# Experts' output bias moved from seventeen small products into the open block sums, as one 24-row product per block

## The chip, the cores and the metric

The kernel runs on one core of one Trainium2 chip. The metric is the device time of one execution in microseconds; the median of three runs of the kernel before is 252.2 us. The core has five engines that run their own instruction queues and wait for each other by semaphores: TensorE (PE, matrix products into the eight banks of PSUM), VectorE (DVE), ScalarE (ACT), GpSimd (POOL) and SyncE (SP), which here only issues transfers. ScalarE and GpSimd issue transfers as well, each on a queue of its own.

## What is computed

A vision transformer block over 32 images: a patch embedding with perturbed weights, a class token, attention with relative positions, and a mixture of eight experts of which each token uses the two with the highest probability. This part matters here (`comb` has one weight for each token and expert, zero for all but two):

```
logits = xf @ Wr.T + br
probs = jax.nn.softmax(logits, axis=-1)
top2_prob, top2_idx = jax.lax.top_k(probs, 2)
comb = jnp.zeros((n, e), x.dtype).at[jnp.arange(n)[:, None], top2_idx].add(top2_prob)
h = jax.nn.gelu(jnp.einsum('nd,edh->enh', xf, W1) + b1[:, None, :], approximate=False)
o = jnp.einsum('enh,ehd->end', h, W2) + b2[:, None, :]
y = jnp.einsum('ne,end->nd', comb, o)
```

The experts' output bias therefore adds `comb @ b2` to each token, a product of (tokens x 8) by (8 x 128). There are 2080 tokens: 2048 patches and 32 class tokens.

## The kernel before

Every engine's program is written out by hand, in the order in which it runs; the order around the change is the order of the calls in the source.

The experts run in two ways. Experts 0 and 1 are "direct". `up(e, blk)` makes the hidden units of one block of 416 tokens (five blocks, `FB` = 416, six products: each operand is split into a rounded high part and a low rest, and three of the four products are taken, for two halves of the hidden units). ScalarE applies the gelu. `down(e, g)` multiplies back for a group of four tiles of 128 tokens (five groups, the last one the class tokens), and DVE adds the result, weighted with the token's weight, to the accumulator `acc` in SBUF (L1286). Each such accumulation counts up `acc_ok`.

Experts 2 to 7 are summed in PSUM. For each of 30 steps (a block and an expert, `STEPS`), PE runs `up`, ScalarE the gelu (`lift`, L760), DVE multiplies the hidden units with the token weights (`weigh`, L1260), ScalarE rounds them to the high part (`rounded`, L768), DVE takes the low rest (`rest`, L1269), and PE adds six products to the block's open sum (`down_sum`), two steps behind the `up`. A sum stays open in bank 4 or 5 over the six experts of a block. ScalarE then copies it out, PE turns it back (`turn_back`, L1836) and DVE adds it to `acc` (`joined`, L1307), after which SyncE and ScalarE write the output.

`weigh` needs each token's weight on all 128 partitions. For that DVE computes the weights `comb` (L1231), PE turns them (`L1789`, after `comb_ok` and the first two accumulations), ScalarE copies them to `combT` and signals `cT_ok`, SyncE and ScalarE write six rows of 2080 weights to a scratch area in the output tensor, and SyncE reads them back with each row repeated over the partitions: one transfer of 208 KB for each expert of block 0 (counted by `d_we2` to `d_we6`), and for each later block one of 832 KB (experts 2 to 5, into `region_c`) and two of 208 KB (expert 6 into `xnT`, expert 7 into `QT`). Block 1's three are counted by `d_wb1`; those of blocks 2, 3 and 4 are counted together, and `weigh` waits for all nine of them:

```
if blk:
    dve.wait_ge(S[f"d_wb{min(blk, 2)}"], 48 if blk == 1 else 3 * 48)
```

The output bias is handled apart. PE forms it from the turned weights with products of 8 rows (`base` in PE's program: sixteen of 128 x 128 between `up(2, 0)` and `up(3, 0)`, one for the class tokens after `up(3, 0)`), into banks that later groups need too, and DVE adds it to `acc` in five instructions (L1239, L1242), before expert 0's last group. In the profile each such product is recorded as two passes, and so is each product of `down`. PE's first open sum waits for all fifteen accumulations, since its banks are among those of the groups.

GpSimd has nothing to do after it has made the second layer norm's scales (L532).

Of the kernel before, what the change touches and what calls it, by code (L numbers as in the profile page):

```python
# [24 lines left out]
E = 8  # L25
# [16 lines left out]
G_RING, H_RING = 4, 6  # L42
BACK = [range(0, 3), range(3, 6), range(6, 9), range(9, 13), range(13, 16)]
# [4 lines left out]
K_ALL = 672  # L48
# [16 lines left out]
def constants():  # L65
# [17 lines left out]
    k[:, K_PRIO:K_PRIO + E] = E - np.arange(E)[None, :]  # L83
    return k


def vit_kernel(nc, consts, x, cls_tok, W1_w, W1_b, W1_sw, W1_sb, W2_w, W2_b, W2_sw, W2_sb, W3_w, W3_b,
               eps_in1, eps_out1, eps_in2, eps_out2, Wq, bq, Wk, bk, Wv, bv, Wo, bo, rel_k, rel_v,
               Wr, br, fW1, fb1, fW2, fb2, out):
    with ExitStack() as ctx:  # L90
# [61 lines left out]
        b2s = sb("b2s", C)  # L152
        clsr = sb("clsr", C)
# [66 lines left out]
        accT = region_d[:, 0:ALL]  # L220

# [15 lines left out]
        names = """d_we2 d_we3 d_we4 d_we6 w2hi_ok w2lo_ok d_cs d_wb1 d_wb2 hs_ok hi_ok lo_ok y3_ps at_ok tb_ps fin_ok nm1_ok nmr1_ok xnA_ok d_const d_const2 d_eo d_w1b d_rows d_bias d_w1 d_w2 d_x0 d_x1 d_x2 d_small d_rel d_rvd d_attn d_ffn d_fw1 d_out d_out2 w1hi_ok w1_split  # L237
# [6 lines left out]
        lg_ok lexp_ok comb_ok cT_ps cT_ok base_ps acc_ok h_ps gelu_ok y2_ps cz_ok lz_ok cb_ok xn2D_ok h0o_ok d_h0s d_h0q nm_ok nmr_ok relkb_ok dve_c dve_m act_c  # L244
# [26 lines left out]
        def out_expert(e, g):  # L271

            n = 5 * e + g
            return n if n < AHEAD else n + 7

        def out_base(c):
            return AHEAD + 2 + c
# [35 lines left out]
        def _(sp_):  # L313
# [66 lines left out]
            sp_.wait_ge(S["d_out"], 16 * 18)  # L380

        @block.gpsimd
        def _(pool):
# [18 lines left out]
            for c in range(4):  # L402
                g.dma_start(b2s[32 * c:32 * c + E, :], fb2).then_inc(S["d_small"], 16)
# [36 lines left out]
            pool.wait_ge(S["d_small"], 112)  # L440
# [85 lines left out]
            g.tensor_tensor(w1_lo[:, :], w1_sb[:, :], w1_hi[:, :].bitcast(F32), ALU.subtract).then_inc(S["w1_split"], 1)  # L526
# [15 lines left out]
            deviation2(4)  # L542

        @block.scalar
        def _(act):
# [244 lines left out]
            for f in range(2, 4):  # L790
                a.dma_start(oq[f][:, tt, :], acc[32 * f:32 * f + 32, tt, :]).then_inc(S["d_out2"], 16)
            act.wait_ge(S["fin_ok"], 6)
            a.dma_start(out[:, 0, :], acc[0:IMG, PAIRS, :]).then_inc(S["d_out2"], 16)
            act.wait_ge(S["d_out2"], 48)

        @block.vector
        def _(dve):
# [69 lines left out]
            dve.wait_ge(S["d_small"], 112)  # L867
# [364 lines left out]
            accv = KT[:, 0:TOK].rearrange("p (g c d) -> p g c d", g=4, c=4)  # L1232

            def base(u):

                dve.wait_ge(S["base_ps"], 1 + u // 4)
                dve.wait_ge(S["acc_ok"], AHEAD)
                if u < 4:
                    v.tensor_tensor(accv[:, :, u], bank[out_bank(out_base(u))].rearrange("p (g d) -> p g d", g=4),  # L1239
                                    accv[:, :, u], ALU.add).then_inc(S["acc_ok"], 1)  # L1240
                else:
                    v.tensor_tensor(acc[0:IMG, PAIRS, :], bank[out_bank(out_base(u))][0:IMG, 0:C], acc[0:IMG, PAIRS, :],  # L1242
                                    ALU.add).then_inc(S["acc_ok"], 1)
# [27 lines left out]
            for e in range(DIRECT):  # L1271
                for g, tiles in enumerate(GROUPS):
                    u = out_expert(e, g)
                    if (e, g) == (0, AHEAD):
                        for c in range(5):
                            base(c)
# [3 lines left out]
                    if e > 0:  # L1280
                        dve.wait_ge(S["acc_ok"], max(AHEAD + 5, out_done(out_expert(e - 1, tiles[0] // 4))))
                    elif g >= AHEAD:
                        dve.wait_ge(S["acc_ok"], AHEAD + 5)
# [6 lines left out]
                    if (e, g) == (1, 2):  # L1290
                        weigh(0)
                        weigh(1)
                    if (e, g) == (1, 3):
                        weigh(2)
                        rest(0)
# [576 lines left out]
```

## Time and profile before

| | |
|---|---|
| measured, three runs | 252.07, 252.2, 254.18 us |
| median | 252.2 us |
| span of the profiled execution, first to last instruction | 249.9 us |
| time around that span | not in the profile |
| PE busy | 230.9 us, 92% of the span |
| DVE busy | 191.3 us, 77% |
| ACT busy | 164.2 us, 66% |
| POOL busy | 62.8 us, 25% |
| granted clock of PE | 1.00 of full speed throughout |

An engine's share is a mean over stages that differ. The last 90 us, from the token weights on, are the stage of the change. PE's records overlap, since products are pipelined: what one costs PE is the step from one start to the next, not its own length.

### The profile page before, as it was taken

To read this page: it belongs to the slowest core of one execution; us is meant where nothing else is said; L and a number is where in the kernel's file an instruction comes from. 1 tells how busy PE (TensorE), PEld (TensorE's weight loads), DVE (VectorE), ACT (ScalarE), POOL (GpSimd) and SP (SyncE) were. 2 spreads that over 40 slices of the span, in tenths; PEclk is the share of its full clock that TensorE was granted. 3 is DMA by queue.
4 is the path that set the end of the run, shared out by engine and by line. 5 is a ranking of instruction groups with operands and counts; after the bars stand their busy time and mean duration, and the time that the engine had idled before them with its cause. 6 is when DMAs were issued, how large, how long until landed. Compare 5 with 4: busy or idle time off the path is not lost.

```text
span 249.9 us, 6298 instructions
## 1 busy us (share of the span) xinstructions
PE 230.9 (92%) x2316; PEld 194.7 (78%) x2316; DVE 191.3 (77%) x481; ACT 164.2 (66%) x509; POOL 62.8 (25%) x94
## 2 busy tenths in 40 slices
PE   1999999999998889989989999999899999999993
PEld 1945665899776766658778899889799999999972
DVE  1576789865668899998186738678999989989991
ACT  2461469752199899993026987422799888898870
POOL 8814132096005465469112400000000000000000
PEclk9999999999999999999999999999999999999999
DMA  6980000000003326064000000069888510001011
GB/s 147 335 217 3 1 0 1 3 3 0 3 0 81 91 65 108 4 212 129 3 7 3 0 3 0 8 103 131 151 211 260 173 37 10 22 4 32 0 42 34
DMA packets 15625, 16.46 MB, mean 66 GB/s; under 512 B 1747, under 2 KB 14367, under 8 KB 15468
## 3 DMA queue, kind: packets, MB, share of 16 engines
q1 hardware_dynamic: 14424, 15.59, 26.0%
q0 software_dynamic: 544, 0.35, 0.6%
q8 instruction: 18, 0.29, 0.5%
q10 hardware_dynamic: 628, 0.14, 0.3%
q14 instruction: 11, 0.09, 0.1%
HBM read 13.91 MB, written 2.16 MB: 64 GB/s over the span
## 4 chain that ended last, share of the span: by engine, by line
PE 54%; DVE 13%; issue 11%; POOL 11%; DMA 4%; ACT 3%; SPq 2%; DVEq 0%; POOLq 0%
PE banks L1328 49%; POOL region_e L471 5%; DMA region_d<-in_L_tok_W_sw 4%; DVE KT L1286 2%; POOL w_lo L526 2%; DVE top L1028 1%; DVE stb L992 1%; POOL region_d L478 1%; PE banks L1531 1%; POOL rstd L413 1%; PE banks L1672 1%; DVE stb L911 1%; ACT region_d L701 1%; DVE y_lo L1269 1%; DVE stats L890 1%
## 5 line engine op out<-in xcount | busy, mean ns | idle before, releaser
L760 ACT ACTIVATE w_sb<-banks,vecs 128x416 f32<-128x416 f32 x60 | 36.4, 608 | 11.2 <-PE banks L1328 8.9
L677 ACT ACTIVATE region_e<-banks,ntop 128x64 f32<-128x64 f32 x128 | 38.3, 346 | 5.0 <-DVE ntop L1035 4.8
L768 ACT ACTIVATE y_hi<-w_sb 128x416 fp32r<-128x416 f32 x60 | 32.7, 548 | 8.1 <-DVE w_sb L1260 8.1
L1269 DVE TENSOR_TENSOR y_lo<-w_sb,y_hi 128x416 fp32r<-128x416 f32 x60 | 34.9, 585 | 1.0 <-ACT y_hi L768 1.0
L677 ACT ACTIVATION_READ_ACCUMULATOR region_e<-banks,ntop 128x1 f32 x128 | 29.8, 238 | 0.0
L1328 PE MATMUL banks<-x_hi,w_hi 128*128 128x416 f32 x80 | 29.3, 366 | 0.0
L1328 PE MATMUL banks<-x_lo,w_hi 128*128 128x416 f32 x80 | 28.1, 352 | 0.0
L1328 PE MATMUL banks<-x_hi,w_lo 128*128 128x416 f32 x80 | 28.0, 350 | 0.0
L1260 DVE TENSOR_TENSOR w_sb<-w_sb,region_c 128x416 f32<-128x416 f32 x40 | 23.4, 586 | 2.5 <-ACT w_sb L760 1.0
L1328 PE MATMUL banks<-y_hi,w_hi 128*128 128x416 f32 x60 | 22.3, 371 | 1.5 <-DVE KT L1286 1.0
L1328 PE MATMUL banks<-y_hi,w_lo 128*128 128x416 f32 x60 | 21.1, 351 | 0.0
L1328 PE MATMUL banks<-y_lo,w_hi 128*128 128x416 f32 x60 | 21.0, 351 | 0.0
L1328 PE MATMUL banks<-kc 128*128 128x128 f32 x76 | 14.1, 316 | 5.6 <-DMA kc<-in_consts 5.6
L471 POOL TENSOR_TENSOR region_e<-region_e,rsum 128x512 f32<-128x512 f32 (+1 forms) x15 | 15.5, 1032 | 7.6 <-DVE ntop L1035 5.6
L1328 PEld LDWEIGHTS banks<-kc 128*128 128x128 f32 x76 | 11.1, 212 | 6.7 <-DMA kc<-in_consts 5.6
L1328 PE MATMUL banks<-w_all,region_d 128*128 128x128 f32 (+1 forms) x136 | 16.3, 277 | 0.0
L1328 PEld LDWEIGHTS banks<-x_hi,w_hi 128*128 128x128 f32 x80 | 15.0, 188 | 1.3 <-DVE x_lo L1168 0.6
L1328 PEld LDWEIGHTS banks<-w_all,region_d 128*128 128x128 f32 (+1 forms) x136 | 15.5, 187 | 0.6 <-ACT w_sb L760 0.2
L1328 PE MATMUL banks<-region_d,relk_bd 64*128 64x64 f32 x256 | 15.3, 288 | 0.0
L1328 PEld LDWEIGHTS banks<-x_lo,w_hi 128*128 128x128 f32 x80 | 15.0, 187 | 0.3
L1328 PEld LDWEIGHTS banks<-x_hi,w_lo 128*128 128x128 f32 x80 | 15.0, 188 | 0.1
L1328 PEld LDWEIGHTS banks<-region_d,relk_bd 64*128 64x128 f32 x256 | 14.6, 188 | 0.6 <-issue 0.5
(238 smaller groups left out, 502.1 us busy)
## 6 DMA issues: line engine op xcount, KB each, us to landing
region_c<-out SPq DMA_DIRECT2D x4, 832.0 KB, 14.3
xnT<-out SPq DMA_DIRECT2D x5, 208.0 KB, 13.7
QT<-out SPq DMA_DIRECT2D x5, 208.0 KB, 14.1
region_a<-in_x SPq DMA_DIRECT2D x2, 512.0 KB, 5.3
region_a<-in_x SPq DMA_DIRECT2D x1, 1024.0 KB, 9.5
out<-h SPq DMA_DIRECT2D x2, 512.0 KB, 5.8
h<-out SPq DMA_DIRECT2D x4, 256.0 KB, 5.0
w_sb<-in_L_ffn_W SPq DMA_DIRECT2D x1, 1024.0 KB, 5.6
```

The lines of the kernel that those rows point to most:

```text
L413: g.tensor_tensor(rstd[:, n * TPB:(n + 1) * TPB], ve[:, n * TPB:(n + 1) * TPB], mhalf[:, :], ALU.pow).then_inc(S["rstd_ok"], 1)
L471: g.tensor_tensor(ev, ev, rv, ALU.mult).then_inc(S["pn_ok"], 1)
L478: g.tensor_copy(pc_rep[:, 2 * (u % 2):2 * (u % 2) + 2, :, :].rearrange("p r h d -> p (r h) d"), PcA[:, 16 * u:16 * u + 16].unsqueeze(2).to ...
L526: g.tensor_tensor(w1_lo[:, :], w1_sb[:, :], w1_hi[:, :].bitcast(F32), ALU.subtract).then_inc(S["w1_split"], 1)
L677: last = a.activation(dst[:, h // 2, h % 2], src[:, h // 2, h % 2], ACT.Exp, scale=SCALE, bias=ntop[:, o + h:o + h + 1], accum_out=esum[:, ...
L701: a.activation(HB[:, e % 2, s, blk * FB:(blk + 1) * FB], bank[h_bank(i)][:, 0:FB], ACT.Gelu, bias=vecs[:, v:v + 1]).then_inc(S["gelu_ok"], 1)
L760: a.activation(lifted(u), bank[h_bank(i)][:, 0:FB], ACT.Gelu, bias=vecs[:, b:b + 1])\
L768: a.activation(h_hi(u), lifted(u), ACT.Copy).then_inc(S["hi_ok"], 1)
L1260: v.tensor_tensor(lifted(u), lifted(u), weights(e)[:, blk * FB:(blk + 1) * FB], ALU.mult)\
L1269: v.tensor_tensor(h_lo(u), lifted(u), h_hi(u).bitcast(F32), ALU.subtract).then_inc(S["lo_ok"], 1)
L1286: last = v.scalar_tensor_tensor(acc[0:m, t, :], bank[out_bank(u)][0:m, i * C:(i + 1) * C], comb[0:m, t, e:e + 1], acc[0:m, t, :], op0=ALU. ...
L1328: return t_.matmul(o, l, r, start=start, stop=stop)
```

## The change

The seventeen bias products, DVE's five additions and their counts go. In their place each block's open sum gets one more product at its end, with 24 rows and 416 columns: the turned weights of the block's tokens (24 rows) by the bias (24 rows by 128). The 24 rows are three times the eight experts, so that the product in the rounded format is as exact as the others: rounded weights by rounded bias, rounded weights by the bias's rest, the weights' rest by the (rounded) bias.

- GpSimd builds the 24 rows of the bias (`b2r`) after its last old work. One added column of the constant table holds the signs for that.
- GpSimd splits the token weights next to `comb`, in place: rounded weights twice, then the rest. PE's transposes now wait for that (`cs_ok`) instead of for `comb_ok`; they turn the 24 new columns along with the eight old ones, so their number stays.
- After `y2_ps` has reached 7 (group 1 of expert 1 is through PE), GpSimd writes the 24 turned rows to the scratch area in five transfers, waits, reads them back in one transfer as 24 rows of 2080 (`crow`), waits, and casts the rows of each block into one of three buffers (`share`).
- PE waits for the block's cast before the added product (`split_ok`).
- With the bias banks gone, the groups use their banks in a new order, expert 1 waits for fewer accumulations, the first open sum waits for the accumulation of expert 1's group 2 in place of the last one, and DVE's first weighings and rests move forward by one group.
- At the end SyncE waits for all 21 output transfers; ScalarE no longer waits for its own three.

The core of the diff:

```diff
-            for c in range(4):
-                g.dma_start(b2s[32 * c:32 * c + E, :], fb2).then_inc(S["d_small"], 16)
+            for c in range(3):
+                g.dma_start(b2s[E * c:E * c + E, :], fb2).then_inc(S["d_small"], 16)
...
+            link(g.tensor_copy(b2t, b2s[0:3 * E, :]))
+            link(g.tensor_scalar(b2n, b2t.bitcast(F32), kc[0:3 * E, K_NM:K_NM + 1], None, ALU.mult))
+            g.tensor_tensor(b2r[0:3 * E, :], b2s[0:3 * E, :], b2n, ALU.add).then_inc(S["split_ok"], 1)
+            cb = comb[:, 0:NT, 0:E]
+            pool.wait_ge(S["comb_ok"], 1)
+            link(g.tensor_copy(comb[:, 0:NT, E:3 * E].rearrange("p t (r e) -> p t r e", r=2).bitcast(F32R),
+                               cb.unsqueeze(2).to_broadcast([P, NT, 2, E])))
+            g.tensor_tensor(comb[:, 0:NT, 3 * E:4 * E].bitcast(F32R), cb, comb[:, 0:NT, E:2 * E], ALU.subtract)\
+                .then_inc(S["cs_ok"], 1)
+            pool.wait_ge(S["d_h0q"], 64)
+            pool.wait_ge(S["cT_ok"], 2)
+            pool.wait_ge(S["y2_ps"], 7)
+            for c in range(4):
+                g.dma_start(scratch((E - DIRECT) * ALL + c * P, [[ALL, 3 * E], [4 * P, 4], [1, P]]),
+                            combT[32 * c + E:32 * c + 4 * E, 0:4 * P].rearrange("e (g m) -> e g m", g=4))                    .then_inc(S["d_crow"], 16)
+            g.dma_start(scratch((E - DIRECT) * ALL + TOK, [[ALL, 3 * E], [1, IMG]]),
+                        combT[E:4 * E, 4 * P:4 * P + IMG]).then_inc(S["d_crow"], 16)
+            pool.wait_ge(S["d_crow"], 16 * 5)
+            g.dma_start(crow, scratch((E - DIRECT) * ALL, [[ALL, 3 * E], [1, ALL]])).then_inc(S["d_crow"], 16)
+            pool.wait_ge(S["d_crow"], 16 * 6)
+            for blk in range(5):
+                if blk >= SHARES:
+                    pool.wait_ge(S["y3_ps"], 6 * (blk - SHARES) + 6)
+                g.tensor_copy(share(blk), crow[:, blk * FB:(blk + 1) * FB]).then_inc(S["split_ok"], 1)
...
                 if k == 0:
                     pe.wait_ge(S["w2hi_ok"], 1)
                     pe.wait_ge(S["w2lo_ok"], 3)
-                    pe.wait_ge(S["acc_ok"], 15)
+                    pe.wait_ge(S["acc_ok"], out_done(out_expert(1, 2)))
+                    pe.wait_ge(S["split_ok"], 2)
...
-                    last = mm(o, w2_hi[:, w], h_lo(u), False, e == E - 1 and s == 1)
+                    last = mm(o, w2_hi[:, w], h_lo(u), False, False)
+                if e == E - 1:
+                    pe.wait_ge(S["split_ok"], 3 + blk)
+                    last = mm(o, b2r[0:3 * E, :], share(blk), False, True)
                 last.then_inc(S["y3_ps"], 1)
```

On PE, after the transposes of the token weights, the kernel before has this order from its bias products on (`comb_all` is the turned weights, `x_hi` and `x_lo` the operand of `up`, `w_all` and `region_d` those of `down`):

```order
L1328 MATMUL banks<-b2s,comb_all 128x128 [waits acc_ok,cT_ok,d_small]
L1328 MATMUL banks<-b2s,comb_all 128x128 x15
L1328 MATMUL banks<-x_hi,w_hi 128x416 [waits gelu_ok]
...
L1328 MATMUL banks<-b2s,comb_all 32x128 [waits acc_ok]
L1328 MATMUL banks<-w_all,region_d 32x128 [waits acc_ok,gelu_ok]
L1328 MATMUL banks<-w_all,region_d 32x128
L1328 MATMUL banks<-w_all,region_d 128x128 [waits acc_ok,gelu_ok]
```

In the changed kernel the bias products are gone from that place, and the end of block 0's sum on PE reads as follows (`y_hi` and `y_lo` are the weighted hidden units, `shares` the cast rows):

```order
L1345 MATMUL banks<-y_hi,w_hi 128x416 [waits lo_ok]
L1345 MATMUL banks<-y_hi,w_lo 128x416
L1345 MATMUL banks<-y_lo,w_hi 128x416
L1345 MATMUL banks<-shares,b2r 128x416 [waits split_ok]
L1345 MATMUL banks<-x_hi,w_hi 128x416 [waits gelu_ok]
```

Seventeen products of 128 columns have left the stretch before the sums, and one of 416 columns with a wait of its own stands at the end of each block.

On DVE, the kernel before has this around the first weighings (`KT` is `acc`, `w_sb` the hidden units, `region_c` the spread weights):

```order
L1286 SCALAR_TENSOR_TENSOR KT<-banks,comb_all,KT 128x128 [waits acc_ok,y2_ps]
L1286 SCALAR_TENSOR_TENSOR KT<-banks,comb_all,KT 128x128 x3
L1260 TENSOR_TENSOR w_sb<-w_sb,region_c 128x416 [waits d_we3,gelu_ok]
L1269 TENSOR_TENSOR y_lo<-w_sb,y_hi 128x416 [waits hs_ok,hi_ok]
L1286 SCALAR_TENSOR_TENSOR KT<-banks,comb_all,KT 32x128 [waits acc_ok,y2_ps]
```

and the changed kernel this:

```order
L1281 TENSOR_TENSOR w_sb<-w_sb,region_c 128x416 [waits d_we2,gelu_ok] x2
L1302 SCALAR_TENSOR_TENSOR KT<-banks,comb_all,KT 128x128 [waits acc_ok,y2_ps]
L1302 SCALAR_TENSOR_TENSOR KT<-banks,comb_all,KT 128x128 x3
L1290 TENSOR_TENSOR y_lo<-w_sb,y_hi 128x416 [waits hs_ok,hi_ok]
L1281 TENSOR_TENSOR w_sb<-w_sb,region_c 128x416 [waits d_we3,gelu_ok]
L1290 TENSOR_TENSOR y_lo<-w_sb,y_hi 128x416 [waits hs_ok,hi_ok]
```

The first two weighings stand one group earlier, and two rests and the third weighing stand before expert 1's group 3 in place of behind it.

## Rows read from the trace of the kernel before

**Rows 1.** Chain that ended last: start us, us, engine, output, line.

```profile
155.95 0.31 DVE comb_all L1231
158.66 0.63 PE banks L1789 x4
...
176.36 16.39 PE banks L1328 x84
...
201.87 0.58 DVE w_sb L1260
```

**Rows 2.** Time line, DVE and PE's weight loads, first weighings of blocks 1, 2.

```profile
186.04 0.59 DVE L1260 TENSOR_TENSOR w_sb<-w_sb,region_c 128x416 f32<-128x416 f32 x1 [0.16 <-ACT w_sb L760]
...
200.85 0.59 DVE L1260 TENSOR_TENSOR w_sb<-w_sb,region_c 128x416 f32<-128x416 f32 x1 [0.83 <-DMA QT<-out]
...
203.01 0.19 PEld L1328 LDWEIGHTS banks<-y_hi,w_hi 128*128 128x128 f32 x1 [0.47 <-DVE y_lo L1269]
```

**Rows 3.** Time line of SyncE's queue: start and length of issues of the broadcast.

```profile
162.53 1.79 SPq L362 DMA_DIRECT2D region_c<-out  x4
...
169.91 2.00 SPq L369 DMA_DIRECT2D QT<-out  x1
...
189.89 1.40 SPq L369 DMA_DIRECT2D QT<-out  x1
```

**Rows 4.** Transfers issued at 169.91 and at 189.89: KB, us to landing.

```profile
QT<-out SPq DMA_DIRECT2D x1, 208.0 KB, 14.8
...
QT<-out SPq DMA_DIRECT2D x1, 208.0 KB, 10.9
```

**Rows 5.** Time line of PE, 162 to 180 us.

```profile
162.18 0.35 PE L1328 MATMUL banks<-x_lo,w_hi 128*128 128x416 f32 x1
...
163.81 0.45 PE L1328 MATMUL banks<-x_hi,w_hi 128*128 128x416 f32 x1
...
164.86 0.35 PE L1328 MATMUL banks<-x_lo,w_hi 128*128 128x416 f32 x1
...
165.48 8.52 PE L1328 MATMUL banks<-w_all,region_d 128*32 128x128 f32 x72
173.93 0.45 PE L1328 MATMUL banks<-x_hi,w_hi 128*128 128x416 f32 x1
...
176.36 0.43 PE L1328 MATMUL banks<-y_hi,w_hi 128*128 128x416 f32 x1 [1.03 <-DVE KT L1286]
...
179.53 0.35 PE L1328 MATMUL banks<-y_hi,w_hi 128*128 128x416 f32 x1
```

**Rows 6.** Time line of DVE, 171 to 179 us.

```profile
171.69 1.12 DVE L1286 SCALAR_TENSOR_TENSOR KT<-banks,comb_all,KT 128x128 f32<-128x128 f32 x4 [0.66 <-PE banks L1328]
...
178.04 0.57 DVE L1260 TENSOR_TENSOR w_sb<-w_sb,region_c 128x416 f32<-128x416 f32 x1
178.54 0.57 DVE L1269 TENSOR_TENSOR y_lo<-w_sb,y_hi 128x416 fp32r<-128x416 f32 x1
```

**Rows 7.** Groups by line, GpSimd: busy us, mean ns; idle before.

```profile
L478 POOL COPY region_d<-rel_rows 128x256 f32<-128x256 f32 x8 | 3.2, 398 | 0.1
...
L392 POOL DMA_DIRECT2D rel_rows<-in_L_attn_rel_k x1 | 0.9, 937 | 0.0
```

**Rows 8.** Busy time by stretch; the last two columns are DMA share and GB/s.

```profile
168.00:170.00 2.00, 2.00 (x20) 2.00 (x20) 1.98 (x7) 0.00 (x0) 0.00 (x0) 1.00 1.00 131
...
178.00:180.00 2.00, 2.00 (x12) 1.98 (x12) 1.87 (x5) 1.65 (x4) 0.00 (x0) 1.00 0.68 118
```

**Rows 9.** Time line of GpSimd and DVE at 109 us.

```profile
109.14 1.04 POOL L471 TENSOR_TENSOR region_e<-region_e,rsum 128x512 f32<-128x512 f32 x1 [1.19 <-DVE rsum L1009]
...
109.29 1.44 DVE L1016 TENSOR_TENSOR region_e<-region_e,rsum 128x512 f32<-128x512 f32 x1
```

**Rows 10.** Transfers issued by GpSimd in the first 11 us: KB, us to landing.

```profile
rows<-in_L_ffn_b POOLq DMA_DIRECT2D x1, 8.0 KB, 4.3
...
rel_rows<-in_L_attn_rel_k POOLq DMA_DIRECT2D x1, 0.5 KB, 7.1
```

More of the change, by code:

```diff
@@ L220, in vit_kernel, with share @@
         accT = region_d[:, 0:ALL]
+        crow = region_d[0:3 * E, ALL:2 * ALL]
+        shares = ctx.enter_context(nc.sbuf_tensor("shares", [3 * E, SHARES * FB], F32R))
+        def share(blk):
+            return shares[:, FB * (blk % SHARES):FB * (blk % SHARES + 1)]
+        b2t = y_hi[0:3 * E, 0:C]
+        b2n = tmpx[0:3 * E, 0:C]
         def weights(e):
@@ L273, in out_expert @@
             n = 5 * e + g
-            return n if n < AHEAD else n + 7
-        def out_base(c):
-            return AHEAD + 2 + c
+            return n if n < AHEAD else n + 2
         def out_done(u):
@@ L790, in _ @@
             for f in range(2, 4):
-                a.dma_start(oq[f][:, tt, :], acc[32 * f:32 * f + 32, tt, :]).then_inc(S["d_out2"], 16)
+                a.dma_start(oq[f][:, tt, :], acc[32 * f:32 * f + 32, tt, :]).then_inc(S["d_out"], 16)
             act.wait_ge(S["fin_ok"], 6)
-            a.dma_start(out[:, 0, :], acc[0:IMG, PAIRS, :]).then_inc(S["d_out2"], 16)
-            act.wait_ge(S["d_out2"], 48)
+            a.dma_start(out[:, 0, :], acc[0:IMG, PAIRS, :]).then_inc(S["d_out"], 16)
         @block.vector
@@ L1289, in _ @@
                     last.then_inc(S["acc_ok"], 1)
-                    if (e, g) == (1, 2):
+                    if (e, g) == (1, 1):
                         weigh(0)
                         weigh(1)
-                    if (e, g) == (1, 3):
+                    if (e, g) == (1, 2):
+                        rest(0)
                         weigh(2)
-                        rest(0)
+                        rest(1)
                 if e == 0:
@@ L1769, in down @@
                 last.then_inc(S["y2_ps"], 1)
-            def base(c, g, m=P):
-                r = slice(32 * c, 32 * c + E)
-                o = bank[out_bank(out_base(c))][0:m, g * P:(g + 1) * P] if g < 4 else bank[out_bank(out_base(4))][0:m, 0:C]
-                return mm(o, combT[r, g * P:g * P + m], b2s[r, :])
             pe.wait_ge(S["d_ffn"], 16)
@@ L1793, in _ @@
             up(DIRECT, 0)
-            pe.wait_ge(S["d_small"], 112)
+            up(DIRECT + 1, 0)
+            down(0, 4)
+            down(1, 0)
             pe.wait_ge(S["cT_ok"], 2)
-            pe.wait_ge(S["acc_ok"], AHEAD)
-            for g in range(4):
-                for c in range(4):
-                    last = base(c, g)
-            last.then_inc(S["base_ps"], 1)
-            up(DIRECT + 1, 0)
-            pe.wait_ge(S["acc_ok"], AHEAD + 1)
-            base(0, 4, IMG).then_inc(S["base_ps"], 1)
-            down(0, 4)
-            for g in range(5):
+            for g in range(1, 5):
                 down(1, g)
```

43 lines of the change are left out of this document (16 added, 27 removed).

## The prediction, made before the change was timed

> **What bounds the kernel now.** I read the chain that ended last first, then the time lines of TensorE (PE) and VectorE (DVE) where the diff cuts in, then the issues and landings of the weight broadcast. The chain [rows 1] shows three things. The token weights are written at 155.95, in 0.31 us; their transposes start at 158.66, so 2.4 us later, held by the accumulation of expert 0's first two groups and not by the weights. From 176.36 PE runs the open block sums, 84 matmuls of 416 columns in 16.39 us, 0.195 us each. And at 201.87 the chain leaves PE for DVE's weighing (L1260). That last row is where the prediction is decided. The first weighing of block 2, at 200.85, had waited 0.83 us for a transfer, and PE lost 0.47 us behind it at 203.01 [rows 2]. The transfer is the last one of SyncE's broadcast: issued at 189.89, landed 10.9 us later, at 200.8 [rows 3, 4]. All weighing of blocks 2 to 4 waits for one count that this landing completes. Likewise the last piece for block 1 was issued at 169.91 and landed 14.8 us later, at 184.7; its block's first weighing was at 186.04, 1.3 us after it. So in the profile of before PE sets the time, and the broadcast is only just ahead of it.
>
> **What the removed steps give.** The sixteen bias products and their wait stand on PE between the last up product at 162.18 and the next at 163.81: 1.63 less the 0.19 of that product itself is 1.44 us. The seventeenth stands between 164.86 and 165.48: 0.62 less 0.19 is 0.43 us [rows 5]. Together 1.87 us of PE. Everything of expert 1 moves up by that, since PE is bound there: its 72 recorded passes (four of them expert 0's last group) run from 165.48 to 173.93, 0.117 us each. Group 1 of expert 1 (36 passes) is then ready at 169.7 - 1.9 = 167.8, group 2 (52) at 169.7. DVE's five additions go too. What DVE does next is now: accumulate group 1 (1.12 us [rows 6], to 168.9), two weighings of 0.5 us each (the step from 178.04 to 178.54), accumulate group 2 (to 171.1), then rest, weigh, rest (to 172.6). PE's up product that stood at 173.93 comes at 172.1 and ends at 173.2, and the first open sum follows at once; before, it started at 176.36, after 1.03 us of waiting for expert 1's last accumulation, and now it waits for two groups fewer. The next limit is DVE: groups 3 and 4 (1.4 us), then five steps of 0.5 us, to 176.6; there the second half of the second open sum can start, which before started at 179.53, just after the rest at 178.54. **PE's lead is 2.9 us.** Were nothing else late, the end would move by -2.9, by five added products of 0.195 (+0.98), and by the stall of 0.47 that goes: -2.4 us.
>
> **Where the lead goes.** The broadcast does not move with PE. It starts from the turned token weights, and the transposes that make them wait for the same accumulation as before, provided that GpSimd's split is done by then. PE's queue behind that wait holds all of expert 1 and the sums. The split is two operations, of 272 and 136 elements a partition; GpSimd's copy of 256 took 398 ns [rows 7], so some 0.43 for the first and, with two inputs, about as much for the second: done at 157.2, 1.4 us before 158.66. I put it at nothing; what it took beyond that cover would come onto the broadcast and so onto the end. Then DVE reaches block 1's first weighing at 186.04 - 2.9 = 183.1 and waits until 184.7: the lead is 1.3 us. It reaches block 2's at 200.0 - 1.3, plus 0.2 for block 0's added product, 198.9, and waits until 200.8: the lead is nothing. From there everything stands as before, and four of the five added products (blocks 1 to 4, since the row at 203.01 belongs to block 1's last expert) lie on the path: 4 x 0.195 = **+0.8 us**. The wait for the broadcast is what comes late in place of PE.
>
> **What the new transfers cost.** The rows written and the rows fetched are 24 x 2080 x 4 bytes = 195 KB each. The broadcast moves 6 pieces of 208 KB and four times 832 + 416 KB, 6240 KB, from 162.53 to 200.8: 163 KB per us. 390 KB at that rate are 2.4 us, the upper end; the lower end is nothing. A gain I exclude, since no issue or piece of the broadcast is removed or moved up. The writes fall at about 168 to 176, where the engines are taken for 1.00 of their time; the fetch after it meets 0.68 [rows 8]. If 0.32 of some four us (1.3 us) is free, that takes back the half that is written and a little of the rest; I take **+0.8 us**, nearer the lower end.
> The Trainium skill's page "DMA: Bandwidth & Descriptors", section "Issuing engines are not separate DMA queues", says that transfers started by GpSimd run on the same 16 engines as SyncE's and interleave with them. Taken strictly, the whole 2.4 us would lengthen the broadcast and the time would be 255.6, inside the forecast's own range. The row at 0.68 leaves room, so I don't take it whole.
>
> **What GpSimd's casts cost.** Five casts of 24 x 416. DVE's product of 128 x 512 at 109.29, which ran beside a product of GpSimd, took 1.44 us [rows 9]; the weighing of 128 x 416 at 178.04, with GpSimd idle, took 0.57, which is 0.70 for 512 columns. So a cast may hold up DVE by up to 0.75 us. Four come before the wait at 200.8, which hides them; one comes after block 1's sum. Between 0 and 0.75 I take **+0.2 us**, since a cast has one input and 416 columns on 24 partitions where that product had two inputs.
>
> **Will the rows be there in time?** PE waits for block 0's share behind its last expert, and everything on PE is queued behind that wait: block 1's up products, and through them ScalarE's and DVE's. DVE's wait until 184.7 and the four steps after it put that point at 184.7 + 2.0 + 3 x 0.195 = 187.3. GpSimd is released by group 1 of expert 1, at 167.8; an issue costs up to 0.94 us (the dearest row [rows 7]), five up to 4.7; a transfer of its queue landed 4.3 to 7.1 us after its issue in the busy first stretch [rows 10]; then a fetch, the same again, and a cast of some 0.7. Earliest, with issues at half that cost, 167.8 + 2.4 + 4.3 + 0.5 + 4.3 + 0.7 = 180.0; latest 167.8 + 4.7 + 7.1 + 0.9 + 7.1 + 0.7 = 188.3. That is 1.0 over the need and still inside the 1.3 us that the wait at 200.8 takes anyway. Nothing, then. The changed waits at the end (SyncE counts all 21 output transfers, ScalarE none) and the constant table's extra column move no instruction on the path: nothing.
>
> **The sum.** The profiled span is 249.9 us; the profile gives no time around it, and the measured median, 252.2, is 2.3 us more. 0.8 + 0.8 + 0.2 = +1.8: span 251.7, measured **254.0 us**. Bounds of the forecast: +0.8 (no traffic, no cast) to +0.8 + 2.4 + 0.75 = +3.95, that is 253.0 to 256.1.
>
> **Rivals.**
> *The gate lies earlier than this profile shows.* The landing at 200.8 is late by only 0.83 us; if in the timed executions it came 3 us earlier, and block 1's 1.6 us earlier, the lead would be kept: 252.2 - 2.4 = 249.8. In part, anything from there to 252.5. For it: the share of the engines falls well below 1 in the middle of the stream, so its end is not fixed by bytes alone. Against: the same queue issues it from the same event, and there is now more traffic, not less. Chance 0.17.
> *The shares come late.* The writes and the fetch lie one behind the other, so each us by which a landing exceeds some 7.2 counts twice. At 9 us the cast ends at 192.1; less the need at 187.3 and the 1.3 that is hidden, +3.5 on the +1.8: 257.5. At the 14.8 us of SyncE's own queue it would be some 15 us. For it: engines at 1.00 in that stretch. Against: SyncE's long landings are in good part its own pieces in a row, and GpSimd's queue has only these six. Chance 0.13, most of it between 255.5 and 258.
> *The change brings PE no lead at all*, because DVE or the split holds the first open sum. Then the same landings decide, and the time is the forecast's; it needs no chance of its own.
>
> **How the numbers follow.** Forecast 0.70, gate earlier 0.17, shares late 0.13. One per cent, 2.5 us, is about what a measurement of this kernel can tell from no change: faster means under 249.7, slower over 254.7. Faster: a third of the first rival, 0.06. Slower: the late shares, 0.13, and somewhat under a third of the forecast, 0.21: 0.34. The rest, 0.60, is within 1%. For 8 in 10 the range leaves out the lower half of the first rival and the upper half of the second, and some spread of the forecast: 250.6 to 256.6. The forecast's own range is 253.0 to 256.1.
>
> **What the new profile would show.** Right: the first open sum starts 3 us earlier, near 173.3, with no wait for accumulation; DVE waits about 1.6 us for a transfer at block 1's first weighing and about 2 at block 2's, which comes at or after 200.8; PE's stalls stand there and no longer at 176; the added product takes 0.2 us a block and never waits. Wrong: the transposes start after 159 (the split is late); PE waits at the share of block 0; or block 2's first weighing waits for ScalarE and not for a transfer, and the span ends before 248.

## The result, and the profile after

The changed kernel took 261.31 us, the median of four runs (260.47 to 263.78), beside 252.13 for the kernel before on the same chip. The ratio is 1.0389, with a 95% interval of 1.0337 to 1.0442. It is slower by 9.2 us, outside the range given. Some executions, whatever the kernel, come out one or more per cent longer, most of them at a lower granted clock, and the medians of the experiments below leave these out. The profiled execution is the run of 263.78; its span is 261.8 us. It stands some 1.5 us late already where the token weights are written (157.49 against 155.95 in [rows 1]). That is within the spread of the traces of this case (155.20 to 157.61 for the same instruction), so its times are compared with 1.5 taken off.

The chain that ended last, from the transposes on (start, length, what):

```profile
160.20 0.63 PE banks L1800 x4
...
160.96 8.61 PE banks L1345 x64
...
170.26 0.77 POOL out L566
171.04 1.74 POOL out L566 x3
172.78 11.23 DMA out<-comb_all
...
184.29 11.79 DMA region_d<-out
...
196.13 0.53 POOL shares L576
196.70 6.30 PE banks L1345 x19
```

In [rows 1] the chain went over PE and DVE here. Now it leaves PE for GpSimd, runs through a write of 11.2 us and a fetch of 11.8, one behind the other, through a cast, and comes back to PE only at 196.70. The issues of that stretch with their landings (KB each, us from issue to landing) say the same, where [rows 10] had 4.3 and 7.1:

```profile
region_d<-out POOLq DMA_DIRECT2D x1, 195.0 KB, 11.8
out<-comb_all POOLq DMA_DIRECT2D x4, 48.0 KB, 10.5
out<-comb_all POOLq DMA_DIRECT2D x1, 3.0 KB, 11.2
```

PE's time line there (start, length; in brackets the idle time and what ended it):

```profile
188.87 0.35 PE L1345 MATMUL banks<-y_lo,w_hi 128*128 128x416 f32 x1
196.70 0.71 PE L1345 MATMUL banks<-shares,b2r 24*128 24x416 f32 x1 [7.48 <-POOL shares L576]
197.34 0.71 PE L1345 MATMUL banks<-x_hi,w_hi 128*128 128x416 f32 x1
...
201.32 0.55 PE L1345 MATMUL banks<-y_lo,w_hi 128*128 128x416 f32 x1
201.67 0.39 PE L1345 MATMUL banks<-x_hi,w_hi 128*128 128x416 f32 x1
```

PE stood for 7.48 us at block 0's share, with block 1's up products queued behind the wait. Then the products come at the lower clock: the twelve steps from 197.34 to 201.67 take 4.33 us where twelve of 0.19 are 2.28, so another 2 us or so. (The first of the twelve, 0.51 us, is the step behind the added product, which is longer at the full clock too.) The windows show the clock (PEclk) in that order, first PE idle, then the lower level:

```profile
core 0: us, PE busy (x) PEld busy (x) DVE busy (x) ACT busy (x) POOL busy (x), PEclk, DMA share, GB/s
...
188.00:192.00 4.00, 1.05 (x5) 0.49 (x3) 2.34 (x5) 1.48 (x4) 0.00 (x0) 0.94 0.78 203
192.00:196.00 4.00, 0.00 (x0) 0.00 (x0) 0.00 (x0) 0.00 (x0) 0.00 (x0) 0.50 0.98 199
196.00:200.00 4.00, 3.30 (x9) 2.83 (x10) 0.57 (x1) 1.22 (x3) 1.96 (x4) 0.50 0.90 270
200.00:204.00 4.00, 4.00 (x20) 3.85 (x19) 2.50 (x6) 2.69 (x7) 0.00 (x0) 0.78 0.53 166
```

Before that, things went as forecast. On GpSimd the split is done at 158.8, ahead of the transposes at 160.20:

```profile
157.86 0.41 POOL L558 CAST comb_all<-comb_all 128x272 fp32r<-128x272 f32 x1 [11.47 <-DVE comb_all L1264]
158.34 0.47 POOL L560 TENSOR_TENSOR comb_all<-comb_all 128x136 fp32r<-128x136 f32 x1
```

The first open sum starts at 174.85, without a wait (173.3 with 1.5 taken off; [rows 5] and the chain of [rows 1] had 176.36):

```profile
174.85 0.35 PE L1345 MATMUL banks<-y_hi,w_hi 128*128 128x416 f32 x1
```

DVE waits at block 1's first weighing, and SyncE's last three issues are later than in [rows 3]:

```profile
186.24 0.59 DVE L1281 TENSOR_TENSOR w_sb<-w_sb,region_c 128x416 f32<-128x416 f32 x1 [1.68 <-DMA QT<-out]
```

```profile
185.52 1.46 SPq L375 DMA_DIRECT2D region_c<-out  x1
187.02 5.46 SPq L378 DMA_DIRECT2D xnT<-out  x1
192.53 1.84 SPq L378 DMA_DIRECT2D QT<-out  x1
```

The last piece was issued at 192.53 (191.0, where before had 189.89). Block 2's first weighing, at 210.40, no longer waits for it, because PE's stand-still came first.

### The profile page after: what moved, and what is told of

Read it like the earlier page. It is cut to its first block, busy times and chain, and to the rows that moved or that the text cites. A ratio compares the mean times of both kernels' runs of the same rounds, so it can differ in the third digit from the quotient of the medians.

```text
span 261.8 us, 6243 instructions
## 1 busy us (share of the span) xinstructions
PE 234.6 (90%) x2287; PEld 196.3 (75%) x2287; DVE 188.8 (72%) x476; ACT 163.8 (63%) x509; POOL 70.7 (27%) x109
## 4 chain that ended last, share of the span: by engine, by line
PE 48%; DMA 13%; POOL 11%; issue 11%; DVE 10%; ACT 3%; SPq 1%; DVEq 0%; POOLq 0%
PE banks L1345 43%; POOL region_e L480 5%; DMA region_d<-out 5%; DMA out<-comb_all 4%; DMA region_d<-in_L_tok_W_sw 4%; POOL w_lo L535 2%; DVE top L1061 1%; DVE stb L1025 1%; POOL region_d L487 1%; POOL out L566 1%; PE banks L1548 1%; POOL rstd L422 1%; DVE KT L1302 1%; PE banks L1689 1%; DVE stb L944 1%
## 5 line engine op out<-in xcount | busy, mean ns | idle before, releaser
L1281 DVE TENSOR_TENSOR w_sb<-w_sb,region_c 128x416 f32<-128x416 f32 x40 | 23.3, 586 | 14.8 <-ACT w_sb L794 12.7
L1345 PE MATMUL banks<-x_hi,w_hi 128*128 128x416 f32 x80 | 30.1, 376 | 0.0
L1345 PE MATMUL banks<-region_b,wnT 128*128 128x512 f32 x32 | 15.0, 602 | 0.1
```

What stands on the lines that cost most here:

```text
L1281: v.tensor_tensor(lifted(u), lifted(u), weights(e)[:, blk * FB:(blk + 1) * FB], ALU.mult)\
L1345: return t_.matmul(o, l, r, start=start, stop=stop)
```

## Experiments

Theory: GpSimd's writes and its fetch stand behind the broadcast that SyncE has already queued, so each lands after 10 to 12 us; PE waits for the shares; and the new transfers delay the broadcast by more than the 0.8 us of the sum. Rivals: the added products or the moved order cost the time; GpSimd's queue is that slow whatever else is queued. Behind each median stand the ratio to the kernel before, measured beside it (medians 251.43 to 252.22 us), and the 95% interval of that ratio.

### The shares not waited for

```diff
+            g.tensor_copy(shares[:, :].rearrange("p (n c) -> p n c", n=12),
+                          b2s[0:3 * E, 0:104].unsqueeze(1).to_broadcast([3 * E, 12, 104])).then_inc(S["split_ok"], 1)
...
-            for blk in range(5):
-                if blk >= SHARES:
-                    pool.wait_ge(S["y3_ps"], 6 * (blk - SHARES) + 6)
-                g.tensor_copy(share(blk), crow[:, blk * FB:(blk + 1) * FB]).then_inc(S["split_ok"], 1)
...
-                    pe.wait_ge(S["split_ok"], 3 + blk)
+                    pe.wait_ge(S["split_ok"], 3)
```

> Changed kernel in which the fetched rows are not used: GpSimd fills the three share buffers early with a constant, the five writes and the fetch stay as they are, the casts go, and the outputs wait for the fetch. The output lacks the right bias. Theory (shares late behind the broadcast): PE no longer stands 7.5 us at block 0's share and keeps its clock; what is left is the broadcast, delayed by the traffic, so the last landing is at about 202 to 204 and the time 253.7 to 256.2 us. Rival 'the added products or the moved order cost the time': it stays within 2 us of 261.

Measured: 257.25 us (1.0161, 1.0087 to 1.0234). The wait for the shares was worth 4.1 us of the 9.2, less than the 7.5 and some 2 that PE lost there, because part of that only covers the next wait. DVE at block 2's first weighing, and PE behind it:

```profile
203.34 0.59 DVE L1281 TENSOR_TENSOR w_sb<-w_sb,region_c 128x416 f32<-128x416 f32 x1 [4.08 <-DMA QT<-out]
```

```profile
204.49 0.46 PE L1345 MATMUL banks<-y_hi,w_hi 128*128 128x416 f32 x1 [2.94 <-DVE y_lo L1290]
```

After those 2.94 us the granted clock fell too: 0.84 in the four microseconds from 204, 0.73 from 208. The ten steps from 206.64 to 210.19 take 3.55 us, where at the full clock one of 0.30 behind the added product and nine of 0.19 would be 2.0, so another 1.5 us. The time lies a little above the forecast range.

### No rows written or fetched

As above, and GpSimd's six transfers and their waits go too.

> As the run before, and the five writes and the fetch are left out as well (the output lacks the right bias). Theory: the broadcast is as in the kernel before, last landing near 200.8, block 2's first weighing waits for it some 2 us, and the time is 252.1 + 0.8 = 252.9 us. Rival 'the gate is not firm': no wait at block 2 and 249.8 us. The difference to the run before is the price of the traffic: 0.8 us by the prediction, up to 3.3 by the trace of the changed kernel.

Measured: 253.23 us (1.0047, 0.999 to 1.0104). Both gates of the prediction (the first weighings of blocks 1 and 2, which wait for a landing) are there, and firm:

```profile
183.70 0.59 DVE L1268 TENSOR_TENSOR w_sb<-w_sb,region_c 128x416 f32<-128x416 f32 x1 [1.22 <-DMA QT<-out]
199.33 0.59 DVE L1268 TENSOR_TENSOR w_sb<-w_sb,region_c 128x416 f32<-128x416 f32 x1 [1.42 <-DMA QT<-out]
```

So with the shares not waited for, the traffic costs 257.25 - 253.23 = 4.0 us (the two intervals overlap a little). The traces agree: block 2's first weighing is at 199.33 here and at 203.34 there, 3.3 us later when the 0.7 by which that execution's split started later, 156.50 against 155.79, is taken off; the 1.5 us of PE's lower clock there come on top, since PE did not stand here for more than 0.26 us. The time is 1.6 us over the 251.63 of the kernel before beside it, where 0.8 was expected; the difference is within the interval. The queues' packets from 160 to 206 us show how the traffic costs (packets, MB, the time they took as a share of 16 engines), first with the transfers, then without:

```profile
q1 hardware_dynamic: 4629, 6.61, 72.8%
q0 software_dynamic: 208, 0.40, 2.6%
```

```profile
q1 hardware_dynamic: 4648, 6.61, 65.0%
```

GpSimd's own packets (q0) take 2.6% of 46 us, 1.2 us of every engine; but SyncE's (q1), nearly as many and the same bytes, take 7.8% more, 3.6 us. The other kept traces in which GpSimd moves no rows have 62.8 to 66.4% in this row, those with GpSimd's fetch 68.0 to 72.8%.

### Released earlier

```diff
-            pool.wait_ge(S["y2_ps"], 7)
+            pool.wait_ge(S["y2_ps"], 5)
```

> Only change: GpSimd writes the rows after the fifth group (y2_ps 5) in place of the seventh, some 3.9 us earlier. Theory: the landings stay at some 10 to 12 us each, since the broadcast is already queued, the shares come 3.9 us earlier, PE's wait at block 0's share falls from 7.5 to about 3.6 us, and the time is about 257 us (256 to 258). Rival 'the lateness is not what costs': 261 us still.

Measured: 256.78 us (1.0156, 1.0084 to 1.0229). The writes went out at 165.10 and landed in 8.8 to 8.9 us, the fetch in 12.4; PE waited 2.0 us at the share, where 3.6 was expected, since the writes landed sooner as well. The time follows the release, as the theory has it. The cost is lateness, and the lateness is made of landings.

### The writes first

```diff
-            pool.wait_ge(S["y2_ps"], 7)
...
             pool.wait_ge(S["d_crow"], 16 * 5)
+            pool.wait_ge(S["y2_ps"], 5)
```

> GpSimd writes the rows as soon as they are turned, at about 162, before SyncE has queued the broadcast (164.1); only the fetch waits for the fifth group. Theory: the writes land in some 3 to 5 us in place of 10.5, the fetch in 8 to 12 behind the first pieces, the shares are there by 182, PE never waits for one, and the time is that of the first run of this set, 253.7 to 256.2 us. Rival 'GpSimd's queue needs 10 us whatever else is queued': writes 10 us, fetch 11 to 12 us, shares at about 188 to 190 and a wait of 0 to 3 us, time 256 to 258 us.

Measured: 254.72 us (1.0108, 1.0056 to 1.0161). The four writes went out from 160.19, before SyncE's first piece at 161.98; the fifth at 162.71, after it; the fetch at 169.07. Their landings:

```profile
out<-comb_all POOLq DMA_DIRECT2D x4, 48.0 KB, 2.1
...
out<-comb_all POOLq DMA_DIRECT2D x1, 3.0 KB, 6.1
```

```profile
region_d<-out POOLq DMA_DIRECT2D x1, 195.0 KB, 11.0
```

The same queue and the same bytes, 2.1 us in place of 10.5. A transfer of 3 KB that came just after the first pieces needed 6.1. The shares were cast at 180.1, and PE did not wait for one. The time is 1.5 us over the run without rows, not 4.0, though all the bytes come from GpSimd's queue and the fetch runs inside the broadcast.

### The broadcast held back

```diff
+            sp_.wait_ge(S["d_crow"], 16 * 6)
             for blk in range(1, 5):
                 b = slice(blk * FB, (blk + 1) * FB)
```

> SyncE issues block 0's six pieces and then waits until the fetched rows have landed, before it issues the rest of the broadcast; GpSimd's transfers are as in the changed kernel. What is read are their landings. Theory (they were slow because the broadcast was already queued): 2 to 4 us for the writes and for the fetch, against 10.5 and 11.8. Rival (GpSimd's own queue is that slow): 8 to 12 us again. The time is no measure here, since the broadcast starts some 12 us later: about 257 to 264 us.

One run, 262.51 us. The landings:

```profile
region_d<-out POOLq DMA_DIRECT2D x1, 195.0 KB, 3.4
out<-comb_all POOLq DMA_DIRECT2D x4, 48.0 KB, 5.5
out<-comb_all POOLq DMA_DIRECT2D x1, 3.0 KB, 4.9
```

The fetch took 3.4 us where it had taken 11.8; the writes, which still met the end of block 0's pieces, 4.9 to 5.5, a little over what was expected. The rival "GpSimd's own queue is that slow" falls. DVE's work is not the cause either: it was busy for all of the 8 us from 168 and for 3.87 of the 4 from 176, while these transfers landed.

### The rows with the six

```diff
-                sp_.dma_start(scratch(c * P, [[ALL, E - DIRECT], [4 * P, 4], [1, P]]),
-                              combT[32 * c + DIRECT:32 * c + E, 0:4 * P].rearrange("e (g m) -> e g m", g=4))\
+                sp_.dma_start(scratch(c * P, [[ALL, 4 * E - DIRECT], [4 * P, 4], [1, P]]),
+                              combT[32 * c + DIRECT:32 * c + 4 * E, 0:4 * P].rearrange("e (g m) -> e g m", g=4))\
...
+            sp_.wait_ge(S["y2_ps"], 5)
+            sp_.dma_start(crow, scratch((E - DIRECT) * ALL, [[ALL, 3 * E], [1, ALL]])).then_inc(S["d_crow"], 16)
             for blk in range(1, 5):
...
+            pool.wait_ge(S["d_crow"], 16)
             for blk in range(5):
```

> The 24 rows are written together with the six (30 rows in the same five transfers of SyncE and ScalarE), and SyncE fetches them right after block 0's pieces; GpSimd issues no transfer and only casts. Theory: the shares are there by about 178, PE never waits for one; the 390 KB stay in the traffic, so block 2's first weighing still waits for the broadcast, and the time is that of the run with the writes first, 253.5 to 256 us. Rival 'the traffic costs only where it is a second queue': 252.5 to 253.5 us.

Measured: 252.43 us (1.0041, 1.0001 to 1.0080), just under the rival's bounds (252.5 to 253.5) and a microsecond under the theory's. SyncE's fetch goes out at 167.12, and GpSimd casts from 177.06 on:

```profile
167.12 1.61 SPq L374 DMA_DIRECT2D region_d<-out  x1
```

```profile
177.06 3.56 POOL L568 CAST shares<-region_d 24x416 fp32r<-24x416 f32 x3 [19.73 <-DMA region_d<-out]
```

From the issue of SyncE's own fetch to the cast behind its landing are 9.9 us. So behind the queued pieces a transfer of 195 KB is not much quicker from SyncE's queue than from GpSimd's, and what makes the shares timely here is that writes and fetch are issued early. The 390 KB are still moved, and the time is no longer than without them (253.23). What cost 4.0 us was therefore not the bytes by themselves. Whether it was GpSimd's queue or the later moment is not settled. Counted from the writing of the token weights, the last landing lets block 2's first weighing go after 44.3 us here, 43.9 without rows, 44.9 in the kernel before, 47.2 in the run in which the shares are not waited for, and 44.7 with the writes first, where the fetch came from GpSimd's queue too, but at 169 in place of 182.

### Counts by piece

```diff
+        FIRST = (None, ("d_wb1", 16), ("d_wb2", 16), ("d_rvd", 32 + 16), ("d_fw1", 16 + 16))
+        REST = (None, ("d_const2", 16 + 32), ("d_w0", 32 + 32), ("d_w2", 32 + 32), ("d_x2", 16 + 32))
...
-                    dve.wait_ge(S[f"d_wb{min(blk, 2)}"], 48 if blk == 1 else 3 * 48)
+                    dve.wait_ge(S[(FIRST if e < 6 else REST)[blk][0]], (FIRST if e < 6 else REST)[blk][1])
```

> As the run before, and each block's weighings wait only for their own pieces (one count for the piece of experts 2 to 5 and one for those of 6 and 7, for each block), not for all nine of blocks 2 to 4. Theory (PE's 2.9 us of lead are eaten only by these counts): the waits at blocks 1 and 2 go, and the time falls to 249.8 us plus the casts, 249.5 to 251 us, below the kernel before. Rival 'a block's own first piece is as late as the count': 252.5 us or more.

Measured: 251.73 us (0.9999, 0.9965 to 1.0032), above the forecast. The waits did go: from 176 us on DVE waits for no transfer, and block 1's first weighing is at 183.91. And yet PE has no 2.4 us over the kernel before. Its time line at block 0's end shows why:

```profile
186.85 0.35 PE L1340 MATMUL banks<-y_lo,w_hi 128*128 128x416 f32 x1
187.13 0.45 PE L1340 MATMUL banks<-shares,b2r 24*128 24x416 f32 x1
187.51 0.46 PE L1340 MATMUL banks<-x_hi,w_hi 128*128 128x416 f32 x1
187.81 0.35 PE L1340 MATMUL banks<-x_hi,w_lo 128*128 128x416 f32 x1
```

From the product ahead to the second behind are 0.28 + 0.38 + 0.30 = 0.96 us. Without the added product they would be two ordinary steps, 0.38. It costs 0.58 us, three times the 0.195 of the sum. A second, smaller loss is DVE beside GpSimd's casts, three in a row from 177.29 (3.54 us in all; in the changed kernel, with DVE idle, four took 1.96):

```profile
178.19 0.57 DVE L1285 TENSOR_TENSOR y_lo<-w_sb,y_hi 128x416 fp32r<-128x416 f32 x1
178.89 0.71 DVE L1276 TENSOR_TENSOR w_sb<-w_sb,xnT 128x416 f32<-128x416 f32 x1
179.53 0.91 DVE L1285 TENSOR_TENSOR y_lo<-w_sb,y_hi 128x416 fp32r<-128x416 f32 x1
180.36 0.91 DVE L1276 TENSOR_TENSOR w_sb<-w_sb,xnT 128x416 f32<-128x416 f32 x1
181.20 0.58 DVE L1285 TENSOR_TENSOR y_lo<-w_sb,y_hi 128x416 fp32r<-128x416 f32 x1
```

Three operations of DVE grew by 0.14 + 0.34 + 0.34 = 0.8 us, of which PE lost 0.22, at 181.83.

### The same counts in the kernel before

The edit of the run above, applied to the kernel before.

> The kernel before with the same counts by piece and nothing else. Theory: the only wait there was 0.83 us at block 2, of which PE lost 0.47, so the time falls by 0 to 0.5 us, within what can be measured. Rival 'the count costs the kernel before as much as the changed one': 1.5 to 2.5 us faster.

Measured: 251.15 us (0.9983, 0.9944 to 1.0021): nothing that can be measured, as expected. Together with the last run below it shows that the counts bind only once PE is ahead.

### 128 rows

```diff
+            link(g.tensor_scalar(b2r[:, :], bob[:, :], 0.0, None, ALU.mult))
+            link(g.tensor_scalar(shares[:, :].rearrange("p (n c) -> p n c", n=12),
+                                 bob[:, 0:104].unsqueeze(1).to_broadcast([P, 12, 104]), 0.0, None, ALU.mult))
...
-                    last = mm(o, b2r[0:3 * E, :], share(blk), False, True)
+                    last = mm(o, b2r[:, :], wide(blk), False, True)
```

`wide(blk)` is `share(blk)` over all 128 rows.

> As the run with counts by piece, and the added product takes 128 rows in place of 24: rows 24 to 127 of the bias and of the share buffers are zeroed once by GpSimd, in its idle time ahead of the token weights. The result is the same. In the run before the step from the last ordinary product over the added one to the second product after it was 0.28 + 0.38 + 0.30 = 0.96 us, where three ordinary steps are 0.57: an added product costs some 0.57 us a block and not 0.195. Theory (the change of rows from 128 to 24 and back costs it): the step falls to 0.19, five blocks give back 1.5 to 1.9 us, and the time is 249.9 us (249.5 to 250.5). Rival (the wait for the share, though long fulfilled, breaks the row of products): steps as before and 251.8 us.

Measured: 250.54 us (0.9958, 0.9928 to 0.9988), faster than the kernel before by 1.2 us (its median was 251.76; the interval is 0.1 to 0.7%) and than the changed one by 10.8. The steps are ordinary ones:

```profile
187.88 0.35 PE L1346 MATMUL banks<-y_lo,w_hi 128*128 128x416 f32 x1
188.07 0.35 PE L1346 MATMUL banks<-shares,b2r 128*128 128x416 f32 x1
188.26 0.35 PE L1346 MATMUL banks<-x_hi,w_hi 128*128 128x416 f32 x1
```

The wait for the share is still in front of the product, so it was not the wait. Against the run with 24 rows the medians differ by 1.2 us, under the 1.5 to 1.9 expected, and the time is at the upper end of the forecast. The gain over the kernel before holds for the moved bias and the counts together. That the moved bias gains anything beyond the counts is not shown: the kernel before with the same counts has 0.9983, and the two intervals overlap.

### The fetch alone, the writes alone

Both start from the first run (shares not waited for). In one the five writes go, and the fetch waits for the fourth step of block 0:

```diff
-            for c in range(4):
-                g.dma_start(scratch((E - DIRECT) * ALL + c * P, [[ALL, 3 * E], [4 * P, 4], [1, P]]),
...
-            pool.wait_ge(S["d_crow"], 16 * 5)
-            g.dma_start(crow, scratch((E - DIRECT) * ALL, [[ALL, 3 * E], [1, ALL]])).then_inc(S["d_crow"], 16)
+            pool.wait_ge(S["d_cs"], 16 * 5)
+            pool.wait_ge(S["y3_ps"], 4)
+            g.dma_start(crow, scratch(0, [[0, 3 * E], [1, ALL]])).then_inc(S["d_crow"], 16)
```

> As the run in which the shares are not waited for, with the fetch alone: no writes, the fetch (of other rows of the scratch area, same 195 KB) issued after the fourth step of block 0, at about 182 us as there; the output lacks the right bias. With both the time was 257.25, with neither 254.16. Theory of the prediction (half of the traffic's price is the writes, the fetch meets engines with room): 254.0 to 254.7 us. Rival (the price is a second queue's transfer in the last third of the broadcast): 256 us or more.

Measured: 254.70 us (1.0117, 1.0041 to 1.0193), at the upper bound of the theory and under the rival. (The fetch reads the first of the six rows 24 times.) In the other the fetch goes and the writes stay.

> As the run in which the shares are not waited for, with the five writes alone and no fetch (the output lacks the right bias). Theory of the prediction: the writes fall where the engines are taken for 1.00 of their time, 255.4 to 257 us. Rival (the fetch is what delays the broadcast): 254 to 254.7 us.

Measured: 253.15 us (1.0043, 1.0001 to 1.0085), under both, nearer the rival. SyncE's packets from 160 to 206 us, first with the fetch alone, then with the writes alone:

```profile
q1 hardware_dynamic: 4648, 6.61, 68.5%
```

```profile
q1 hardware_dynamic: 4648, 6.61, 64.6%
```

With neither it was 65.0%, with both 72.8%. The writes cost nothing that can be seen. The fetch costs something, by this row 3.5% of 46 us, 1.6 us; the times, 1.5 us between the fetch alone and neither, don't settle it, since their intervals overlap. That both together cost more than the fetch alone stays unexplained.

### 128 rows with the old counts

The run with 128 rows, without `FIRST` and `REST`.

> As the run with 128 rows, with the counts of the changed kernel back (one for block 1's three pieces, one for all nine of blocks 2 to 4). Theory (the counts eat PE's lead): block 1's first weighing waits some 1.5 us and block 2's 0.5 to 2 us for the broadcast, and the time is 251.5 to 252.5 us, no better than the kernel before. Rival (with 128 rows the counts no longer bind): 250.5 us as with counts by piece.

Measured: 252.00 us (1.0024, 0.9980 to 1.0069), as expected. DVE waits again, 0.70 us at block 1 (1.5 was expected) and 2.20 at block 2:

```profile
183.97 0.59 DVE L1279 TENSOR_TENSOR w_sb<-w_sb,region_c 128x416 f32<-128x416 f32 x1 [0.70 <-DMA QT<-out]
200.01 0.59 DVE L1279 TENSOR_TENSOR w_sb<-w_sb,region_c 128x416 f32<-128x416 f32 x1 [2.20 <-DMA QT<-out]
```

So the counts are worth some 1.5 us in this form (the two intervals overlap a little; the waits stand in one trace and not in the other). With them PE's lead is lost, and with it the gain of the whole change.

## Why the prediction was wrong

The 9.2 us, by differences of medians:

| part | predicted | measured | from |
|---|---|---|---|
| gates and added products | +0.8 | +1.1 | run without rows, less before (252.13) |
| traffic | +0.8 | +4.0 | shares not waited for, less without rows |
| shares late (casts included) | +0.2 | +4.1 | changed kernel, less shares not waited for |

By the median that the kernel before had beside the run without rows (251.63), the first row is +1.6; each row is good to a microsecond or so. The second holds some 1.5 us of PE's lower clock. How the cost falls on the last two rows depends on what is taken away first: with the writes first nothing is late, the same bytes are moved from the same queue, and the time is 254.72, so that the lateness would be 6.6 us and the traffic 1.5.

**The failed step is "Will the rows be there in time?"** It took a landing of 4.3 to 7.1 us from [rows 10], a stretch in which GpSimd's transfers met SyncE's first loads (2.43 MB in 11 us) but no broadcast, found the shares ready by 188.3 at the latest, and put the lateness at nothing. The transfers landed after 10.5 (four of the writes), 11.2 (the fifth) and 11.8 (the fetch), the first cast ended at 196.66, and PE stood for 7.48 us. The other numbers of the step held: GpSimd was released about when expected (at 170.26, 168.8 with 1.5 taken off, against 167.8), the five issues took 3.1 us, inside 2.4 to 4.7, and PE reached the wait near the 187.3 worked out (188.87 plus a step, less 1.5). Nearer rows lay in [rows 4]: 10.9 and 14.8 for SyncE's own pieces in the same stretch. I set them aside because those are "its own pieces in a row"; the run with the broadcast held back (3.4 us), the one with the writes first (2.1 us) and SyncE's own fetch in the run with the six (9.9 us to the cast) show that what is queued at the moment of issue decides, whichever of the two engines issues.

The Trainium skill's page "DMA: Bandwidth & Descriptors", section "Issuing engines are not separate DMA queues", says that transfers of either engine run on the same 16 engines and interleave. The prediction used that for the price of the traffic alone and not for the landings. The trace agrees that the two affect each other: SyncE's packets took 72.8% of the engines' time with GpSimd's transfers among them and 65.0% without. That a later transfer would be served at once is not in the measurement: 3 KB took 11.2 us behind the broadcast and 6.1 just after its first pieces.

**The rival "the shares come late" was the right mechanism**, with 0.13 where it deserved the largest chance. Its own arithmetic, with the measured landings, gives 196.66 - 1.5 - 187.3 = 7.9 us of waiting, where the trace has 7.5. Its time was still too low: most of its chance lay between 255.5 and 258, for landings near 9 us. What it lacked is the clock, some 2 us more at the lower level after the stand-still.

**The added product was sized at 0.195 us, that of a 128-row product, and cost 0.58.** I took the ordinary step and set no bound above it, though a nearer row was in [rows 5]: the seventeenth bias product, one of 8 rows among products of 128, took 0.43 us, which I counted on the side that was removed and not on the side that was added. (Without it the step at that place is still 0.28 in the changed kernel, so taking it out gave 0.34.) Four of them on the path make 2.3 us, not 0.8; the first row of the table is lower, but the interval of the run without rows reaches 1.04%, 2.6 us. Five make 2.9, as much as the whole lead that PE won. So even without any gate and with the rows there in time (counts by piece) the 24-row product gains nothing; with 128 rows the gain is 1.2 us. The Trainium skill's page "TensorEngine Tiling (Array Packing)", section "Key Properties", says that a change of the tiling mode drains the engine. The steps of 0.28, 0.38 and 0.30 at the 24-row product, and 0.19 with 128 rows, agree with that; the trace doesn't name the mode.

**The traffic was sized at 0.8 us between 0 and 2.4, and cost 4.0 with the fetch at 182**, of which some 1.5 are PE's clock. The upper bound counted bytes at the broadcast's own rate; but SyncE's packets themselves took longer, by 3.6 us, while GpSimd's transfers ran. The room that the prediction gave the fetch is that of one row, 0.68 at 178 to 180 [rows 8]; in the same view of the kernel before, the stretches of 2 us from 180 to 192 have 0.83 to 0.97. And the halves were the other way about, as far as the packets show it: the writes, put where the engines were full, cost nothing to be seen, the fetch does.

**What held:** the split hidden (done at 158.8, transposes at 160.20); the first open sum 3.0 us earlier and without a wait (173.3 against 176.36); the wait of 1.6 us at block 1 (1.68); the gate at block 2 (1.42 us of waiting without the traffic, 4.08 with it); the counts as what eats PE's lead (252.00 with them, 250.54 without, both with 128 rows). The casts reach 0.8 us of DVE when they run beside it, just over the upper bound of 0.75, but little of it reaches PE. The rival with an earlier gate had no part in it: DVE waited 1.22 and 1.42 us at the two gates even without rows.

## What to carry to other kernels

A small transfer on which an engine will wait took, in this case, about as long as the stream's own pieces that were already queued for the DMA engines when it was issued. Take its landing from a row of the same stretch, and issue it before the large stream or early in it. Count a product of fewer rows between full ones by its neighbours' steps too; padding it with zero rows can be cheaper, as it was here (0.19 us for 0.58). And before a lead is won on one engine, look for the counts that lump several transfers together: they bind only once the lead is there, and give it back.

## What the hardware did that I had not expected

- The landing of GpSimd's transfers went from 2.1 us (48 KB, ahead of the broadcast) to 10.5 (the same transfers, some 8 us later), and of the 195 KB fetch from 3.4 us to 12.4.
- SyncE's 6.61 MB took 72.8% of the 16 engines' time in 46 us with GpSimd's transfers among them, 65.0% without; with the same rows issued by SyncE and ScalarE it was 66.3% for 6.91 MB, and they cost nothing that was measured. What in the engines makes the difference was not found.
- A product of 24 rows costs 0.58 us among products of 128 rows; the same product with 128 rows, 0.19.
- After PE had stood for 7.5 us, its clock was granted at 0.50 (1.2 GHz) and the step of a product was 0.35 us from 197.85 to 201.67. After 2.94 us of standing in another run the four-microsecond means fell to 0.84 and 0.73, and the steps were 0.35 us from 207.08 to 209.85.
